# Flamingo block on one core: a table of its own for the last batch but one, a router without the softmax's sum, later weight splits and later reads of the counts

## The chip, the cores and the metric

The kernel is one program on one core of a Trainium2 chip. The metric is the device time of one execution in microseconds (us), as a median over several. Five engines work side by side: TensorE (PE, with its weight loads shown apart as PEld), VectorE (DVE), ScalarE (ACT), GpSimd (POOL) and SyncE (SP, which issues most DMAs). They wait for each other by semaphores alone.

## The reference, cut to what matters

Eight batches of 112 query rows (D = 256) go through four residual steps. `_L1_ffn_ref` is the part that the change touches most.

```python
x = x + tanh(g_xattn[0]) * _L0_xattn_ref(_layernorm(x), ctx, ...)   # 16 heads of 16
x = x + tanh(g_ffn[0]) * _L0_ffn_ref(_layernorm(x), ...)            # three matrices, tanh
x = x + tanh(g_xattn[1]) * _L1_xattn_ref(_layernorm(x), ctx, ...)   # 8 heads of 64, keys of x and ctx
x = x + tanh(g_ffn[1]) * _L1_ffn_ref(_layernorm(x), ...)            # 8 experts, 2 of them per row

def _L1_ffn_ref(hidden_states, gate_w, gate_up_proj, down_proj):
    probs = jax.nn.softmax(x @ gate_w.T, axis=-1)
    w, idx = jax.lax.top_k(probs, 2)
    w = w / jnp.sum(w, axis=-1, keepdims=True)
    ...   # for each expert: acc + ce * (silu(x @ g.T) * (x @ u.T)) @ dn.T
```

The two weights of a row are divided by their own sum, so the softmax's sum cancels in them.

## The kernel before, in words

`attention_order` writes out both attention layers as one list of stages. Each stage has a time in tables such as `PAIR`, `PREP1`, `TAIL1`, `TAIL_LAST` and `SPLIT`; the list is sorted by these times, and every engine walks the same list and does its share of each stage in that order. The times only set an order; nothing waits for a clock. A stage that comes early in the list and isn't ready holds up all that its engine has behind it.

In the second layer each batch has four pairs of heads. A pair is `S` (scores on PE, L667; maxima on DVE, L1034; exponentials on ACT, L1440), `sc` (POOL divides by the sums, all batches but the last), `T` (eight transposes on PE, L683; copies on ACT, L1140, and DVE, L1142) and `V` (values on PE, L701). The last batch is not divided before `V`: `rv` and `rb` (L712) bring the reciprocals of its sums, and `aT` (L1055) multiplies them in.

A tail follows each batch: `wo` (PE, L743), `res` (DVE, L1081 and L1087), `stats`, `norm` (DVE, L981, after POOL's rstd), `xt` (transposes, L482), `xtc` (ACT copy, L1318) and the router. The router is `rt0` (logits, L762), `rt1` (maximum and difference on DVE, exponential on ACT, L1476), `rt2` and `rt3` (one-hot rows `o1` and `o2` of the two best experts; each small DVE instruction waits for the one before through the semaphore `rchain`), `rt4` (weights on DVE; on PE the running places of the rows by a triangular and an all-ones matrix, L770 and L771) and `rt5` (row numbers `i1` and `i2` on DVE; two indirect DMAs on POOL, L1663, which scatter the 112 rows and their copy to the experts' places in DRAM). Every batch's tail but the last one's stands by `TAIL1` behind the last pair of its attention. So the tail of batch 6 (the last but one) lies among the four pairs of batch 7.

`keep_warm` puts spare transposes into PE's queue at fixed places (`WARM`): 18 ahead of the last `xt`, 26 ahead of the last `rt4`, 56 ahead of the first expert's `xin`.

The expert stage (`expert_order`) begins when all rows are scattered: SP waits for all the indirect DMAs, loads an expert's rows, PE transposes them (`xin`, L794), ACT and DVE make a high and a low half (L1493, L1227), and PE multiplies by weights that are split into high halves (ACT, L1566) and low halves (DVE, L1298, which reads the raw weights and the high half). Each expert has six such chunks. The six of expert 0 are split at the places of `SPLIT`; chunks 0 to 3 hold the first matrix, 4 and 5 the second. The weights of expert 0 are asked for by SP (L1780) behind the last `v1` of the attention. Each engine reads the number of rows of each expert from SBUF into registers (`count_of`, L863), for branches that handle more than 256 rows of an expert.

Of the kernel before, what the change touches and what calls it, by code (L numbers as in the profile page):

```python
# [10 lines left out]
ALU = mybir.AluOpType  # L11
ACT = mybir.ActivationFunctionType
AX = mybir.AxisListType
# [66 lines left out]
def emptied_by(stage, *i):  # L80
# [4 lines left out]
    if stage in ("kp", "v"):  # L85
# [45 lines left out]
         (33.31, "rt5"))  # L131
TAIL_LAST = ((1.58, "rv"), (4.84, "rb"), (6.92, "rbc"), (8.1, "aT"), (9.72, "wo"), (10.67, "res", 3),
# [3 lines left out]
SPLIT = ((4.0, 0), (4.72, 1), (6.9, 2), (15.65, 3), (15.74, 4), (22.13, 5))  # L136


WARM = {("kp", 0, 1, 0): 36, ("spk", 0, 0): 26, ("spk", 0, 2): 24, ("xt", NB - 1, 3): 18, ("rt4", NB - 1): 26, ("xin", 0): 56}


def attention_order():

    order, timed = Order(), []
    TQ, TP, TL = 5.5, 6.4, 4.4
    T1 = TQ * NQUAD + 4

# [36 lines left out]
    return order  # L186
# [53 lines left out]
def build(nc, A, out):  # L240
    ctx = ExitStack()
    with ctx:
# [102 lines left out]
        R = {n: sb("r_" + n, [NQ, NB, NE]) for n in ("p", "e1", "o1", "e2", "o2", "p2", "m", "t", "u")}  # L345
        r1 = {n: sb("q_" + n, [NQ, NB]) for n in ("mx", "z", "v1", "v2", "a", "b", "s1", "s2", "d")}
# [120 lines left out]
        def tensor_attention(e, w):  # L467
# [6 lines left out]
            for stage, *i in order.entries:  # L474
# [669 lines left out]
        def vector_route(e, w, stage, b):  # L1144
            r = {n: R[n][:, b, :] for n in R}
            q = {n: r1[n][:, b:b + 1] for n in r1}
            c = 24 * b
# [6 lines left out]
            elif stage == "rt2":  # L1154
                w.wait_ge(s("rexp"), b + 1)
                e.tensor_reduce(q["z"], r["u"], AX.X, ALU.add).then_inc(s("rchain"), 1)
                w.wait_ge(s("rchain"), c + 1)
                e.reciprocal(q["d"], q["z"]).then_inc(s("rchain"), 1)
                w.wait_ge(s("rchain"), c + 2)
                e.tensor_scalar(r["p"], r["u"], q["d"], None, ALU.mult).then_inc(s("rchain"), 1)  # L1160
                w.wait_ge(s("rconst"), 4)
                first_of(e, w, c + 3, r["p"], q["v1"], r["e1"], q["a"], r["o1"])
                w.wait_ge(s("rchain"), c + 7)
                e.scalar_tensor_tensor(r["p2"], r["o1"], -2.0, r["p"], ALU.mult, ALU.add).then_inc(s("rchain"), 1)
            elif stage == "rt3":
                first_of(e, w, c + 8, r["p2"], q["v2"], r["e2"], q["b"], r["o2"])
                w.wait_ge(s("rchain"), c + 12)
                e.tensor_tensor(r["m"], r["o1"], r["o2"], ALU.add).then_inc(s("rchain"), 1)
            elif stage == "rt4":
                e.tensor_tensor(q["s1"], q["v1"], q["v2"], ALU.add).then_inc(s("rchain"), 1)  # L1170
                w.wait_ge(s("rchain"), c + 14)
                e.reciprocal(q["s2"], q["s1"]).then_inc(s("rchain"), 1)
                w.wait_ge(s("rchain"), c + 15)
                for to, v in ((XN[:, b, :], "v1"), (XN2[b], "v2")):
                    e.scalar_tensor_tensor(to[:, D:D + 1], q[v], q["s2"], tg[0:NQ, 3:4], ALU.mult,
                                           ALU.mult).then_inc(s("rchain"), 1)
            else:
# [10 lines left out]
                at = c + 18  # L1188
# [9 lines left out]
        def first_of(e, w, at, src, v, eq, mx, oh):  # L1198

            w.wait_ge(s("rchain"), at)  # L1200
            e.tensor_reduce(v, src, AX.X, ALU.max).then_inc(s("rchain"), 1)
            w.wait_ge(s("rchain"), at + 1)
            e.scalar_tensor_tensor(eq, src, v, dec[:, :], ALU.is_equal, ALU.mult).then_inc(s("rchain"), 1)
            w.wait_ge(s("rchain"), at + 2)
            e.tensor_reduce(mx, eq, AX.X, ALU.max).then_inc(s("rchain"), 1)
            w.wait_ge(s("rchain"), at + 3)
            e.tensor_scalar(oh, eq, mx, None, ALU.is_equal).then_inc(s("rchain"), 1)

        def vector_experts(e, w):
# [9 lines left out]
            count = counts(e, w)  # L1219
            for stage, *i in moe.entries:  # L1220
# [8 lines left out]
                elif stage == "up":  # L1229
# [5 lines left out]
                                    ALU.mult).then_inc(s(f"pair{u % 3}"), 1)  # L1235
                elif stage == "hid":
# [23 lines left out]
                elif stage == "far":  # L1260
                    with e.If(count[NE] > 384):
# [216 lines left out]
        def scalar_experts(e, w):  # L1478
# [4 lines left out]
            count = counts(e, w)  # L1483
            for stage, *i in moe.entries:
# [10 lines left out]
                elif stage == "up":  # L1495
# [3 lines left out]
                    if n >= 2:  # L1499
                        w.wait_ge(s("hid"), n - 1)  # L1500
                    e.activation(SG[:, n % 2, :], ps[:, PAIRS[pair_use[(stage, x, dc)] % 3][0], :],  # L1501
                                 ACT.Silu).then_inc(s("silu"), 1)
                elif stage == "hid":
# [21 lines left out]
                elif stage == "far":  # L1525
                    with e.If(count[NE] > 384):
# [60 lines left out]
        def pool_attention(e, w):  # L1587
            for stage, *i in order.entries:
# [67 lines left out]
                elif stage == "rt5":  # L1656
# [4 lines left out]
                    for z, (i_, rows) in enumerate(((i1, XN[:, b, :]), (i2, XN2[b]))):  # L1661
                        w.wait_ge(s("rchain"), 24 * b + 21 + 3 * z)
                        e.indirect_dma_start(xs, bass.IndirectOffsetOnAxis(ap=i_[:, b:b + 1], axis=0), rows,  # L1663
                                             None).then_inc(s("scatter"), 16)
# [236 lines left out]
```

## Time and profile before

| | |
|---|---|
| runs | 632.99, 634.67, 635.07 us; median 634.67 |
| profiled execution | 632.88 us, its span 631.0 |
| busy share of the span | PE 92%, PEld 77%, DVE 63%, ACT 49%, POOL 45% |
| mean granted TensorE clock | 0.986 of full |
| order of time | first layer to about 212 us, second layer to about 437, last tails to about 459, experts to the end |

The span runs from the first to the last instruction that the profiler saw. A busy PE is not PE at its peak, since its matmuls overlap. The rows that the argument rests on stand in the section ahead of the prediction.

### The profile page before, as it was taken

To read this page: it belongs to the slowest core of one execution; us is meant where nothing else is said; L and a number is where in the kernel's file an instruction comes from. 1 tells how busy PE (TensorE), PEld (TensorE's weight loads), DVE (VectorE), ACT (ScalarE), POOL (GpSimd) and SP (SyncE) were. 2 spreads that over 40 slices of the span, in tenths; PEclk is the share of its full clock that TensorE was granted. 3 is DMA by queue.
4 is the path that set the end of the run, shared out by engine and by line. 5 is a ranking of instruction groups with operands and counts; after the bars stand their busy time and mean duration, and the time that the engine had idled before them with its cause. 6 is when DMAs were issued, how large, how long until landed. Compare 5 with 4: busy or idle time off the path is not lost.

```text
span 631.0 us, 13685 instructions
## 1 busy us (share of the span) xinstructions
PE 583.1 (92%) x5588; PEld 488.9 (77%) x5588; DVE 398.2 (63%) x809; ACT 309.1 (49%) x590; POOL 282.2 (45%) x240
## 2 busy tenths in 40 slices
PE   6779989999988999999999999987789999988994
PEld 5657666676756787878888787866679999987994
DVE  7564576677676465676756666577717777745761
ACT  2245545454544545554554546465125676635541
POOL 5967367558540045446546554630200443311224
PEclk9999999999989999999999999997989999999998
DMA  7900380000000000000000000045071776635111
GB/s 250 351 8 1 134 340 1 2 2 2 2 2 1 2 1 1 8 2 23 16 9 16 9 23 2 23 173 242 22 235 49 239 241 226 209 75 209 29 24 23
DMA packets 24170, 50.92 MB, mean 81 GB/s; under 512 B 7408, under 2 KB 16928, under 8 KB 20768
## 3 DMA queue, kind: packets, MB, share of 16 engines
q1 hardware_dynamic: 18784, 45.33, 20.0%
q0 software_dynamic: 4224, 3.70, 3.3%
q10 hardware_dynamic: 1088, 0.88, 0.5%
q8 instruction: 49, 0.80, 0.5%
q14 instruction: 25, 0.20, 0.1%
HBM read 37.89 MB, written 13.31 MB: 81 GB/s over the span
## 4 chain that ended last, share of the span: by engine, by line
PE 68%; POOL 14%; DVE 11%; ACT 3%; issue 2%; DMA 2%; SPq 0%; POOLq 0%; DVEq 0%; ACTq 0%
PE ps L58 13%; PE ps L60 12%; PE ps L59 12%; POOL sr L1612 11%; PE ps L701 4%; PE ps L667 4%; PE ps L683 4%; DVE KN L1009 4%; PE ps L633 2%; PE ps L647 2%; PE ps L623 2%; PE ps L542 2%; PE ps L561 2%; PE ps L743 2%; DMA WR<-in_gupT 1%
## 5 line engine op out<-in xcount | busy, mean ns | idle before, releaser
L1654 POOL TENSOR_SCALAR P<-P,rinv 112x487 f32<-112x487 f32 x56 | 85.6, 1539 | 63.2 <-DVE rinv L1042 63.0
L1612 POOL TENSOR_TENSOR sr<-sv,mhalf 125x32 f32<-125x32 f32 x16 | 87.0, 5437 | 1.3
L58 PE MATMUL ps<-XGf,WH 128*128 128x256 f32 x256 | 73.4, 287 | 2.8 <-ACT P L1559 1.4
L374 POOL DMA_INDIRECT out<-WS,rows_i x16 | 28.4, 1773 | 103.3 <-ACT WS L1514 99.3
L59 PE MATMUL ps<-XGf,WH 128*128 128x256 f32 x256 | 73.2, 286 | 0.0
L60 PE MATMUL ps<-XGf,WL 128*128 128x256 f32 x256 | 73.1, 286 | 0.0
L1009 DVE TENSOR_REDUCE KN<-ps 112x4 f32<-112x1500 f32 x32 | 55.0, 1719 | 26.3 <-PE ps L542 26.1
L1298 DVE TENSOR_TENSOR WL<-WR,WH 128x1024 fp32r<-128x1024 f32 x48 | 57.5, 1223 | 11.6 <-ACT WH L1566 11.5
L1440 ACT ACTIVATE P<-ps,nm 112x487 f32<-112x487 f32 x64 | 42.1, 663 | 45.3 <-DVE nm L1034 43.8
L1391 ACT ACTIVATE P<-ps 125x1344 f32<-125x1344 f32 x32 | 41.3, 1292 | 43.1 <-PE ps L561 43.1
L58 PEld LDWEIGHTS ps<-XGf,WH 128*128 128x128 f32 x256 | 49.8, 195 | 3.3 <-DVE XGf L1227 1.6
L1034 DVE TENSOR_REDUCE nm<-ps 112x1 f32<-112x487 f32 x64 | 39.3, 655 | 18.8 <-PE ps L667 18.8
L59 PEld LDWEIGHTS ps<-XGf,WH 128*128 128x128 f32 x256 | 49.9, 195 | 0.0
L60 PEld LDWEIGHTS ps<-XGf,WL 128*128 128x128 f32 x256 | 49.9, 195 | 0.0
L1566 ACT ACTIVATE WH<-WR 128x1024 fp32r<-128x1024 f32 x48 | 48.9, 1050 | 0.1
L1234 DVE TENSOR_TENSOR P<-P,ps 128x512 f32<-128x512 f32 x32 | 22.0, 687 | 38.1 <-PE ps L60 38.1
L58 PE MATMUL ps<-HTf,CS 128*125 128x256 f32 (+1 forms) x120 | 44.3, 369 | 0.0
L1018 DVE TENSOR_TENSOR KK<-ps,KK 128x487 fp32r<-128x487 f32 x32 | 21.2, 662 | 29.9 <-ACT KK L1408 29.9
L1501 ACT ACTIVATE P<-ps 128x512 f32<-128x512 f32 x32 | 19.1, 596 | 41.8 <-PE ps L60 41.8
L1599 POOL TENSOR_SCALAR ve<-mv 112x1 f32<-112x1 f32 x24 | 5.5, 231 | 75.7 <-DVE mv L974 75.7
L58 PE MATMUL ps<-WH,HTf 128*128 128x256 f32 x136 | 39.2, 289 | 0.0
L60 PE MATMUL ps<-HTf,CS 128*125 128x256 f32 (+1 forms) x120 | 39.2, 326 | 0.0
(233 smaller groups left out, 1530.1 us busy)
## 6 DMA issues: line engine op xcount, KB each, us to landing
WR<-in_gupT SPq DMA_DIRECT2D x16, 1024.0 KB, 7.2
WR<-in_dwnT SPq DMA_DIRECT2D x8, 1024.0 KB, 10.8
xs<-ZT SPq DMA_DIRECT2D x14, 516.0 KB, 5.8
P<-xs SPq DMA_DIRECT2D x24, 128.0 KB, 9.0
CT<-in_ctxT SPq DMA_DIRECT2D x1, 2250.0 KB, 10.1
Wk<-in_L_xattn_Wk SPq DMA_DIRECT2D x2, 512.0 KB, 10.5
Wv<-in_L_xattn_Wv SPq DMA_DIRECT2D x2, 512.0 KB, 11.0
out<-X SPq DMA_DIRECT2D x8, 112.0 KB, 1.9
```

The costliest lines, as they stand in the source:

```text
L58: e.matmul(out, ah, bh, start=start, stop=False)
L59: e.matmul(out, ah, bl, start=False, stop=False)
L60: return e.matmul(out, al, bh, start=False, stop=stop)
L374: return e.indirect_dma_start(result, rows, src, None, bounds_check=NT - 1, oob_is_err=False, compute_op=ALU.add)
L1009: e.tensor_reduce(heads(KN[b % 2][0:NQ, 3, :])[:, 4 * k:4 * k + 4, 16], ps[0:NQ, 0:4, 0:NC], AX.X, ALU.max, negate=True).then_inc(s("smax" ...
L1034: e.tensor_reduce(nm[:, k:k + 1], ps[0:NQ, z, 0:487], AX.X, ALU.max, negate=True).then_inc(s("nm"), 1)
L1298: e.tensor_tensor(WL[x % 3][:, cs], WR[x % 3][:, cs], f_(WH[x % 2][:, cs]), ALU.subtract).then_inc(s("wl"), 1)
L1391: e.activation(PQ[:, q % 3, :].rearrange("p (g n) -> p g n", g=4), ps[0:125, 0:4, 0:3 * NQ], ACT.Exp).then_inc(s("ex"), 1)
L1440: e.activation(P[:, k, 0:487], ps[0:NQ, z, 0:487], ACT.Exp, bias=nm[:, k:k + 1], accum_out=rsum[:, k:k + 1] if i[0] < LAST_A else rsum_las ...
L1566: e.activation(WH[x % 2][:, cs], WR[x % 3][:, cs], ACT.Copy).then_inc(s("wh"), 1)
L1612: e.tensor_tensor(sr[:, p, :], sv[:, p, :], mhalf[0:125, 0:32], ALU.pow).then_inc(s("sr"), 1)
L1654: e.tensor_scalar(P[:, k, 0:487], P[:, k, 0:487], rinv[:, k:k + 1], None, ALU.mult).then_inc(s("psc"), 1)
```

## The change

Four things change.

1. Batch 6 gets a table of its own, `TAIL_NEXT`: its `xt` and all of its router now stand behind the last `T` of batch 7, and `rt2`, `rt3` and DVE's part of `rt4` stand ahead of batch 7's `res`.
2. The router no longer sums the exponentials or divides by the sum. The best expert is where the difference to the maximum is 0, and its weight is 1, so `o1` needs only DVE. `m` = `o1` + `o2` is no longer made: PE adds the two in PSUM, by four matmuls where there were two. A batch has 19 steps in `rchain` where there were 24.
3. Chunks 3, 4 and 5 of expert 0 are split behind the last `rt5` on DVE, and behind the last exponential of the router on ACT.
4. DVE and ACT no longer read all nine counts ahead of the first expert. They read each one behind dc = 2 of its expert, as PE did already.

```diff
+TAIL_NEXT = ((12.96, "aT"), (14.41, "wo"), (16.12, "res", 3), (18.96, "stats", 3), (23.9, "norm", 3), (24.5, "xt", 3),
+             (25.0, "xtc", 3), (29.1, "rt0"), (29.15, "rt1"), (30.1, "rt2"), (30.2, "rt3"), (30.25, "rt4"),
+             (33.2, "rt5"))
-SPLIT = ((4.0, 0), (4.72, 1), (6.9, 2), (15.65, 3), (15.74, 4), (22.13, 5))
+SPLIT = ((4.0, 0), (4.72, 1), (6.9, 2), (38.0, 3), (38.1, 4), (38.2, 5))
...
-            for d, stage, *i in TAIL_LAST if last else TAIL1:
+            for d, stage, *i in TAIL_LAST if last else TAIL_NEXT if n == 2 * NB - 2 else TAIL1:
...
-                    w.wait_ge(s("rchain"), 24 * b + 13)
-                    e.matmul(ps[0:NQ, bk, 0:8], tri[:, :], R["m"][:, b, :], start=True, stop=True)
-                    t = e.matmul(ps[0:NQ, bk, 8:16], ones[:, :], R["m"][:, b, :], start=True, stop=True)
+                    w.wait_ge(s("rchain"), RC * b + 8)
+                    for cs, mat in ((slice(0, 8), tri), (slice(8, 16), ones)):
+                        for n in ("o1", "o2"):
+                            t = e.matmul(ps[0:NQ, bk, cs], mat[:, :], R[n][:, b, :], start=(n == "o1"), stop=(n == "o2"))
...
             elif stage == "rt2":
+                for sem_, v in emptied(("rt0", b)):
+                    w.wait_ge(sem_, v)
+                w.wait_ge(s("rconst"), 4)
+                e.scalar_tensor_tensor(r["e1"], r["t"], 0.0, dec[:, :], ALU.is_equal, ALU.mult).then_inc(s("rchain"), 1)
+                first_of(e, w, c + 1, r["e1"], q["a"], r["o1"])
+                w.wait_ge(s("rchain"), c + 3)
                 w.wait_ge(s("rexp"), b + 1)
-                e.tensor_reduce(q["z"], r["u"], AX.X, ALU.add).then_inc(s("rchain"), 1)
-                w.wait_ge(s("rchain"), c + 1)
-                e.reciprocal(q["d"], q["z"]).then_inc(s("rchain"), 1)
-                w.wait_ge(s("rchain"), c + 2)
-                e.tensor_scalar(r["p"], r["u"], q["d"], None, ALU.mult).then_inc(s("rchain"), 1)
...
-            count = counts(e, w)
+            count = []
...
+                    if dc == 2:
+                        count.append(count_of(e, w, x))
```

On DVE, behind the last batch's reciprocals, this stood before (S is the scratch that holds `rinv_last`, `rT` and `aT`; L1055 is `aT`, L1081 is batch 7's `res`, L1298 a split; the r_ and q_ names are batch 6's router):

```order
L1298 TENSOR_TENSOR WL<-WR,WH 128x1024 x2
L1151 TENSOR_REDUCE q_mx<-ps 112x1
L1153 TENSOR_SCALAR r_t<-ps,q_mx 112x8
L1142 COPY P<-ps 125x448
...
L1164 SCALAR_TENSOR_TENSOR r_p<-r_o,r_p 112x8
L1055 TENSOR_TENSOR S<-ps,S 128x448
...
L1168 TENSOR_TENSOR r_m<-r_o 112x8
L1298 TENSOR_TENSOR WL<-WR,WH 128x1024
L1081 TENSOR_TENSOR tt<-ps,bias 112x256
```

and this stands there in the changed kernel, whose lines are numbered a little higher (L1063 is `aT`, L1089 is `res`):

```order
L1150 COPY P<-ps 125x448
L1063 TENSOR_TENSOR S<-ps,S 128x448
L1162 TENSOR_REDUCE q_mx<-ps 112x1
L1164 TENSOR_SCALAR r_t<-ps,q_mx 112x8
L1170 SCALAR_TENSOR_TENSOR r_e<-r_t,dec 112x8
...
L1216 TENSOR_SCALAR r_o<-r_e,q_b 112x8
L1183 TENSOR_SCALAR q_s<-q_v 112x1
L1185 RECIPROCAL q_s<-q_s 112x1
L1187 TENSOR_SCALAR XN<-q_s,tg 112x1
L1188 SCALAR_TENSOR_TENSOR S<-q_v,q_s,tg 112x1
L1089 TENSOR_TENSOR tt<-ps,bias 112x256
```

The three splits are gone from here, the copy of the last transposes comes at once, and 14 small router instructions now stand between `aT` and `res`.

On PE, around batch 7's last transposes, before (L762 is batch 6's `rt0`; the lines L683 are the last pair's `T`, L712 is `rb`):

```order
L482 MATMUL ps<-ident,XN 128x112 x2
L762 MATMUL ps<-GW,XT 112x8 x2
L683 MATMUL ps<-ident,P 112x112
...
L712 MATMUL ps<-ident,S 128x112 x4
L701 MATMUL ps<-P,VV 64x112 x16
L743 MATMUL ps<-WO,S 112x256 x4
L770 MATMUL ps<-r_m,sq 112x8
```

and in the changed kernel (L488 is `xt`, L689 `T`, L707 `V`, L768 `rt0`, L749 `wo`, L779 `rt4`):

```order
L689 MATMUL ps<-ident,P 125x112 x3
L718 MATMUL ps<-ident,S 128x112 x4
L488 MATMUL ps<-ident,XN 128x112 x2
L707 MATMUL ps<-P,VV 64x112 x16
L768 MATMUL ps<-GW,XT 112x8 x2
L749 MATMUL ps<-WO,S 112x256 x4
L779 MATMUL ps<-r_o,sq 112x8 x4
```

Batch 6's `xt` and `rt0` moved from ahead of the last `T` to behind it, and `rt4` has four matmuls.

On DVE, behind the last `rt5` (L1208 is the cast to `i2`, L1222 the first of the counts, L1236 the first expert's low half), the changed kernel has:

```order
L1208 CAST i<-q_b 112x1
L1310 TENSOR_TENSOR WL<-WR,WH 128x1024 x3
L1222 TENSOR_TENSOR r_t<-base,ebase 112x8
L1224 CAST cnt<-r_t 112x8
L1225 TENSOR_REDUCE q_d<-r_t 112x1
L1227 CAST cnt<-q_d 112x1
L1236 TENSOR_TENSOR XGf<-ps,XGf 128x512
```

Before, the cast was followed at once by the counts. Now three splits stand between, with no wait in front of them.

## Rows read from the trace of the kernel before

**Rows 1.** The page: share of the span by engine in the chain.

```profile
PE 68%; POOL 14%; DVE 11%; ACT 3%; issue 2%; DMA 2%; SPq 0%; POOLq 0%; DVEq 0%; ACTq 0%
```

**Rows 2.** Windows: us, then busy of PE, PEld, DVE, ACT, POOL; clock; DMA.

```profile
300.00:350.00 50.00, 50.00 (x400) 41.21 (x397) 32.49 (x101) 25.66 (x60) 27.00 (x22) 1.00 0.05 15
```

**Rows 3.** Chain of waits, one inner batch's rt4: start us, us, what.

```profile
307.33 0.29 PE ps L770 x2
307.62 0.20 PE ps L771 x2
```

**Rows 4.** Chain of waits at the weights of expert 0: start us, us, what.

```profile
418.22 7.38 DMA WR<-in_gupT
...
427.85 0.67 DVE nm L1034
```

**Rows 5.** Timeline of PE in the last tails: start us, us, line, tile, shapes, records.

```profile
430.92 1.06 PE L683 MATMUL ps<-ident,P 112*112 112x112 f32 x8
431.91 0.99 PE L701 MATMUL ps<-P,VV 112*64 112x112 f32 x16
...
439.12 3.17 PE L701 MATMUL ps<-P,VV 112*64 112x112 f32 x32
443.02 1.98 PE L743 MATMUL ps<-WO,S 128*112 128x256 f32 x8 [0.73 <-DVE S L1055]
```

**Rows 6.** Timeline of ACT around the last exponentials.

```profile
433.08 0.54 ACT L1140 ACTIVATE P<-ps 125x448 f32<-125x448 f32 x1
...
435.40 0.36 ACT L1318 ACTIVATE XT<-ps 128x224 f32<-128x224 f32 x1
```

**Rows 7.** Timeline of DVE: aT and the first instruction of res.

```profile
442.34 0.62 DVE L1055 TENSOR_TENSOR S<-ps,S 128x448 f32<-128x448 f32 x1 [1.58 <-PE ps L701]
...
445.04 0.42 DVE L1081 TENSOR_TENSOR tt<-ps,bias 112x256 f32<-112x256 f32 x1
```

**Rows 8.** Windows of PE alone: busy, records, granted clock, DMA share, GB/s.

```profile
436.00:437.00 1.00, 1.00 (x6) 0.50 0.02 8
...
466.00:467.00 1.00, 1.00 (x7) 0.50 1.02 155
```

**Rows 9.** Timeline of DVE and PE: the router of batch 7.

```profile
449.91 0.23 DVE L1153 TENSOR_SCALAR r_t<-ps,q_mx 112x8 f32<-112x8 f32 x1
...
451.33 0.23 DVE L1203 SCALAR_TENSOR_TENSOR r_e<-r_p,q_v,dec 112x8 f32<-112x8 f32 x1
...
453.18 0.17 DVE L1168 TENSOR_TENSOR r_m<-r_o 112x8 f32<-112x8 f32 x1
...
449.53 3.04 PE L453 MATMUL ps<-ident 128*128 128x128 f32 x26
453.50 0.33 PE L770 MATMUL ps<-r_m,sq 112*112 112x8 f32 x2 [0.93 <-DVE q_s L1170]
```

**Rows 10.** Timeline of DVE, POOL and PE: from the row numbers to expert 0.

```profile
455.31 0.16 DVE L1213 TENSOR_TENSOR r_t<-base,ebase 112x8 f32<-112x8 f32 x1
...
455.62 0.94 POOL L1663 DMA_INDIRECT xs<-XN,i  x1 [3.76 <-DVE i L1195]
456.86 0.94 POOL L1663 DMA_INDIRECT xs<-S,i  x1 [0.30 <-issue]
...
462.29 0.44 PE L794 MATMUL ps<-ident,P 128*128 128x128 f32 x2 [1.53 <-DMA EX<-xs]
```

**Rows 11.** Timeline of POOL and DVE in the experts: scatters beside splits.

```profile
508.81 1.58 POOL L374 DMA_INDIRECT out<-WS,rows_i  x1 [10.46 <-ACT WS L1514]
510.69 2.24 POOL L374 DMA_INDIRECT out<-WS,rows_i  x1 [0.30 <-issue]
...
509.14 2.37 DVE L1298 TENSOR_TENSOR WL<-WR,WH 128x1024 fp32r<-128x1024 f32 x2 [1.21 <-ACT WH L1566]
```

**Rows 12.** One line's instructions (ns min/median/max), and a window of the experts.

```profile
L863 DVEq TENSOR_LOAD <-cnt x9: 298/309/559, 456.0 to 461.5; - x9
...
490.00:500.00 10.00, 10.00 (x86) 10.00 (x85) 7.91 (x11) 7.91 (x11) 6.57 (x4) 1.00 0.92 328
```

More of the change, by code:

```diff
@@ L343, in build @@
                ((XGf[:, 2560:3584], B["Wk2l"][:, :]), (HTf[:, 2048:3072], B["Wv2l"][:, :]))]
-        R = {n: sb("r_" + n, [NQ, NB, NE]) for n in ("p", "e1", "o1", "e2", "o2", "p2", "m", "t", "u")}
-        r1 = {n: sb("q_" + n, [NQ, NB]) for n in ("mx", "z", "v1", "v2", "a", "b", "s1", "s2", "d")}
+        R = {n: sb("r_" + n, [NQ, NB, NE]) for n in ("e1", "o1", "e2", "o2", "p2", "t", "u")}
+        r1 = {n: sb("q_" + n, [NQ, NB]) for n in ("mx", "v2", "a", "b", "s1", "s2", "d")}
         i1, i2 = sb("i1", [NQ, NB], U32), sb("i2", [NQ, NB], U32)
@@ L1146, in vector_route @@
             q = {n: r1[n][:, b:b + 1] for n in r1}
-            c = 24 * b
+            c = RC * b
             if stage == "rt1":
@@ new lines, in vector_route @@
+                w.wait_ge(s("rconst"), 4)
+                e.scalar_tensor_tensor(r["e1"], r["t"], 0.0, dec[:, :], ALU.is_equal, ALU.mult).then_inc(s("rchain"), 1)
+                first_of(e, w, c + 1, r["e1"], q["a"], r["o1"])
+                w.wait_ge(s("rchain"), c + 3)
+                w.wait_ge(s("rexp"), b + 1)
+                e.scalar_tensor_tensor(r["p2"], r["o1"], -2.0, r["u"], ALU.mult, ALU.add).then_inc(s("rchain"), 1)
+            elif stage == "rt3":
+                w.wait_ge(s("rchain"), c + 4)
+                e.tensor_reduce(q["v2"], r["p2"], AX.X, ALU.max).then_inc(s("rchain"), 1)
+                w.wait_ge(s("rchain"), c + 5)
+                e.scalar_tensor_tensor(r["e2"], r["p2"], q["v2"], dec[:, :], ALU.is_equal,
+                                       ALU.mult).then_inc(s("rchain"), 1)
+                first_of(e, w, c + 6, r["e2"], q["b"], r["o2"])
@@ L1169, in vector_route @@
             elif stage == "rt4":
-                e.tensor_tensor(q["s1"], q["v1"], q["v2"], ALU.add).then_inc(s("rchain"), 1)
-                w.wait_ge(s("rchain"), c + 14)
+                e.tensor_scalar(q["s1"], q["v2"], 1.0, None, ALU.add).then_inc(s("rchain"), 1)
+                w.wait_ge(s("rchain"), c + 9)
                 e.reciprocal(q["s2"], q["s1"]).then_inc(s("rchain"), 1)
[L1173 to L1176, printed above, removed]
+                w.wait_ge(s("rchain"), c + 10)
@@ L1177, in vector_route @@
+                e.tensor_scalar(XN[:, b, D:D + 1], q["s2"], tg[0:NQ, 3:4], None, ALU.mult).then_inc(s("rchain"), 1)
+                e.scalar_tensor_tensor(XN2[b][:, D:D + 1], q["v2"], q["s2"], tg[0:NQ, 3:4], ALU.mult,
+                                       ALU.mult).then_inc(s("rchain"), 1)
             else:
@@ L1187, in vector_route @@
                                 ALU.add).then_inc(bank_sem("rt4", b), 1)
-                at = c + 18
+                at = c + 13
                 for oh, s_, i_ in ((r["o1"], q["a"], i1), (r["o2"], q["b"], i2)):
@@ L1196, in vector_route, with first_of @@
                     at += 3
-        def first_of(e, w, at, src, v, eq, mx, oh):
+        def first_of(e, w, at, eq, mx, oh):
             w.wait_ge(s("rchain"), at)
-            e.tensor_reduce(v, src, AX.X, ALU.max).then_inc(s("rchain"), 1)
+            e.tensor_reduce(mx, eq, AX.X, ALU.max).then_inc(s("rchain"), 1)
             w.wait_ge(s("rchain"), at + 1)
[L1203 to L1206, printed above, removed]
             e.tensor_scalar(oh, eq, mx, None, ALU.is_equal).then_inc(s("rchain"), 1)
@@ L1260, in vector_experts @@
                 elif stage == "far":
+                    count.append(count_of(e, w, NE))
                     with e.If(count[NE] > 384):
@@ L1482, in scalar_experts @@
             w.wait_ge(s("rt4"), NB)
-            count = counts(e, w)
+            count = []
             for stage, *i in moe.entries:
@@ L1502, in scalar_experts @@
                                  ACT.Silu).then_inc(s("silu"), 1)
+                    if dc == 2:
+                        count.append(count_of(e, w, x))
                 elif stage == "hid":
@@ L1525, in scalar_experts @@
                 elif stage == "far":
+                    count.append(count_of(e, w, NE))
                     with e.If(count[NE] > 384):
@@ L1661, in pool_attention @@
                     for z, (i_, rows) in enumerate(((i1, XN[:, b, :]), (i2, XN2[b]))):
-                        w.wait_ge(s("rchain"), 24 * b + 21 + 3 * z)
+                        w.wait_ge(s("rchain"), RC * b + 16 + 3 * z)
                         e.indirect_dma_start(xs, bass.IndirectOffsetOnAxis(ap=i_[:, b:b + 1], axis=0), rows,
```

8 lines of the change are left out of this document (1 added, 7 removed).

## The prediction

> **What bounds the kernel now.** I read the page first. Its chain of the work that ended last is two thirds PE [rows 1], but such a share is a mean over stages, so I asked for windows. Across the second layer PE is busy for the whole of each window and the others are not [rows 2]; the reader sees 50.00 of 50.00 for PE, 32.49 for DVE and 27.00 for POOL. What PE gets more to do there is paid in full. Then I followed the chain of waits piece by piece from 404 us on. At 418.22 PE drops out of it: the load of expert 0's weights takes 7.38 us, ACT and DVE split a chunk of it, and only then come the maxima of a pair, at 427.85 [rows 4]. That load is asked for behind PE's last `v1`, so it moves with PE. From there to the experts the chain alternates between engines, a string of latencies in which a removed wait is a gain. In the experts PE is full again [rows 12].
>
> **The tail of batch 6 (a gain of 4.3 us).** Last exponentials done, ACT copies the previous pair from 433.08 to 433.62, and that copy is the last thing the final `T` needs. But ahead of it in PE's queue stand batch 6's `xt` and `rt0`, and on ACT two splits stand ahead of the copy that `rt0` needs, so that copy begins only at 435.40 [rows 6]. All of this is the wait that the new order removes. PE also runs at half its clock here: 0.50, the level of 1.2 GHz, in the window at 436 [rows 8], behind these waits. `V` shows it: two pairs take 3.17 us for 32 records, where one pair took 0.99 for 16 at full clock, so 1.98 for two [rows 5].
>
> In the new order `T` starts at 433.7. At full clock its eight transposes take 1.0 us and the six behind it (`rb` four, `xt` two) 0.75 at the same rate [rows 5]; with `V` at 1.95 this ends at about 437.3. I assume full clock, since PE then idles only 0.8 us, from the end of `V` at 432.9 [rows 5] to 433.7. The copies and reciprocals that it needs from DVE and ACT have no split in front of them any more. `aT` starts at 437.3 and not at 442.34 [rows 7]: 5.0 us earlier.
>
> Not all of it is kept. Before, `res` started 2.70 us behind the start of `aT` [rows 7], about when `wo` was done, 0.68 + 1.98 behind it [rows 5]; the router steps and a split filled that time on DVE. Now 14 router instructions stand there. Those of batch 7 give their pace: from `r_e` at 451.33 to `r_m` at 453.18 are 8 steps, 0.23 each [rows 9]. Ten such are 2.3 us; the last four wait less for each other, and I take 0.6 for them. With 0.55 for `aT` that is 3.45 in all instead of 2.70. So `res` starts at 440.75 and not at 445.04 [rows 7]: 4.3 us earlier. From `res` to the last `rt0` nothing changes. Bounds: if the clock falls all the same, 1.2 us more for `V`, so 3.1; if the small steps were no longer than `wo`, 5.0.
>
> **The router of batch 7 (a gain of 0.55 us).** `e1` can now follow `r_t` at 450.17 instead of 451.33, which is 1.16 us, and PE waits for `o2` and no longer for `m`, a step of 0.19 behind it: 1.35 us in all [rows 9]. PE can't use all of it. Its 26 spare transposes run from 449.53 to 452.57, while `rt4` began at 453.50 [rows 9]. So 0.95 us is gained there at most, and two matmuls more at 0.20 each give 0.4 back.
>
> **Four matmuls for two (a loss of 2.0 us).** In an inner batch `rt4` takes 0.29 + 0.20 us in the chain [rows 3]: the second matmul, 112 rows by 8 columns, costs 0.20 though it computes almost nothing. Two more per batch are 0.4 us. Batches 0 to 4 pay it while PE is the bound [rows 2]: 5 x 0.4 = 2.0. Batch 5's lies behind the last `v1` and beside the 7.38 us load [rows 4], batch 6's ahead of 18 spare transposes; both are hidden. DVE's five steps fewer per batch gain nothing, since DVE isn't the bound here. Bounds: 1.0 if the repeated matrix costs half, 2.5 if each costs what a half of the 0.49 is.
>
> **Splits in the gap before the experts (a loss of 1.9 us).** DVE has nothing to do from the counts until the first expert's rows are there, so three splits seem free: 3.5 us by their row of two in 2.37 [rows 11], in the 7 us from 455.31 to 462.29 [rows 10]. But POOL issues the last two scatters in the same gap, at 455.62 and 456.86 [rows 10], and every row of expert 0 waits for them. Scatters beside splits have rows in the experts. The one at 508.81, before a split began, took 1.58. The one at 510.69, begun while the second of two splits ran (509.14 to 511.51), took 2.24 [rows 11]: 0.66 more, most of what was left of that split. So a split in progress holds a scatter back until it ends. Laid onto the new order, in the old times: the splits start at 455.31, where the first step of the counts stood [rows 10], and again at 456.45 and 457.6. The first scatter comes at 455.62, is held to 456.4 and ends at 457.35; the second comes 0.30 later at 457.65, just behind the start of the third split, and is held to 458.75. Before it ran at 456.86: 1.9 us later.
>
> The Trainium skill (page "SBUF — State Buffer", section "Who interferes with whom") speaks against this place: a VectorE instruction with two inputs in SBUF contends with a GpSimd instruction that reads SBUF, and the loser blocks for the whole instruction. By that rule, the trace agrees: the lengthened scatters are those that meet a split. The same section also says that its own probe saw `tensor_tensor` not stall a DMA; by this the term would be 0 and the sum 1.9 lower, and the row of 2.24 speaks against it.
>
> **The clock at the experts' start (a loss of 0.5 us).** PE's spare transposes end 1.53 us before the first rows come [rows 10], and a little later the clock is at 0.50 for a few us of dense matmuls [rows 8]. With 1.9 us more of idle time PE starts the experts slow rather than falls slow on the way. I take 0.5 from between 0 (the slow stretch only moves) and 1.5 (it lasts twice as long).
>
> **The counts (0).** Nine reads stood in the same gap, 0.3 us each and 5.5 us from the first to the last [rows 12]; with the splits there they would end after the first rows' arrival, so their move is what pays for the splits' move. In the experts one read costs DVE 0.7 us (5.5 / 8) per expert, and DVE is idle for a fifth of a window there [rows 12]. It reads behind the product of dc = 2, and the next half that PE needs is due one `up` later.
>
> **The sum** is made against the profiled execution (632.88 us): -4.3 - 0.55 + 2.0 + 1.9 + 0.5 = -0.45. That execution lies 1.8 us below the median of the runs, 634.67, so I put the difference on the median: **634.2 us**.
>
> **Rivals.**
> - *Only the first scatter is held.* The second would come 0.02 to 0.12 us behind the start of the third split, which is close; if it gets in first, the loss is 0.8 and the clock's 0.3: -1.75, 632.9 us. For it: the margin. Against: the times as laid out above put it behind.
> - *No scatter is held.* Then -2.85, 631.8. Only the row of 2.24 speaks against it, and that row's scatter adds into the output, another form.
> - *The extra matmuls are free*, since two of the four use a matrix just loaded: -2.45, 632.2. Against: the 0.20 of the second matmul.
> - *POOL does not get in between the splits* (the other side). They follow each other without a wait. No row shows a scatter that arrives in the first of several. If it is held until all three are over, at 458.75, the second scatter starts at 460.0, 3.1 us late, and the clock costs the full 1.5: +1.75, 636.4. It decides from the point where the first scatter has not begun before 456.45. The Trainium skill (same page, section "SBUF: two separate sides") says there are deep queues that would have to be drained to share; by that this rival would be the outcome, and I give it a seventh.
> - *The clock falls in the last attention too*: +1.2, so +0.75, 635.4.
>
> **How the numbers follow.** Forecast 35 in 100, first scatter only 25, starved POOL 15, none held 10, free matmuls 8, clock in the tail 7. What a measurement can tell from no change is about 0.3%, 1.9 us. The forecast and the tail clock lie within it; the first-only case lies at its edge and gives half of its chance to faster; none held and free matmuls are faster; the starved case is half slower. With some spread on each: faster 0.34, same 0.50, slower 0.16. The range runs from none held, with the gain a little above, to the starved case: 631.4 to 636.6.
>
> **What would show it.** In the changed kernel's profile: the last `T` within 1 us of the last exponentials and a granted clock of 1.00 at the two `V`s; `res` 4 to 5 us earlier against the last maxima; the four matmuls of the last `rt4` in 0.9 us and a distance from the first to the sixth `rt4` that is 2.0 us longer; PE's `rt4` of batch 7 straight behind the spare transposes; the first scatter of batch 7 longer than 1.5 us and the second longer than 1.9. If the scatters take 0.94 the term of 1.9 is wrong; if the last `v1` comes no later than before, the 2.0 is wrong; if DVE's counts make PE wait in an expert, the 0 is.

## The result, and the profile after

The changed kernel takes 637.07 us (median of 12 runs, 635.36 to 638.67), the kernel before 634.57 us beside it (12 runs, 632.43 to 637.53). The ratio is 1.0040, with a 95% interval of 1.0024 to 1.0056: 2.5 us slower, where 0.5 us faster was forecast and the range ended at 636.6. The top of its page, whose rows answer to [rows 1]:

```profile
span 635.1 us, 13717 instructions
PE 588.7 (93%) x5620; PEld 492.9 (78%) x5620; DVE 391.0 (62%) x769; ACT 308.6 (49%) x590; POOL 287.8 (45%) x240
PEclk9979999999999999999999999999979999989998
PE 70%; POOL 13%; DVE 10%; ACT 3%; issue 2%; DMA 1%; SPq 0%; POOLq 0%; DVEq 0%; ACTq 0%
```

The shares tell little: PE is busy for 93% as before. The clock line has a 7 in the third of its 40 slices (from 32 us on), a 7 in the 30th, where the experts start, and an 8 in the 36th, in the overflow of expert 4. All three come up again below.

**The last attention** (PE's timeline; V is L707, T is L689, `wo` is L749) answers to [rows 5 to 7]:

```profile
436.32 0.99 PE L707 MATMUL ps<-P,VV 112*64 112x112 f32 x16
438.14 1.03 PE L689 MATMUL ps<-ident,P 112*112 112x112 f32 x8 [0.83 <-ACT P L1148]
439.67 1.76 PE L707 MATMUL ps<-P,VV 112*64 112x112 f32 x32
442.16 1.98 PE L749 MATMUL ps<-WO,S 128*112 128x256 f32 x8 [0.24 <-DVE S L1063]
```

The last T follows 0.5 us behind the last exponentials, which end at 437.6, and the two V take 1.76 us for 32 records instead of 3.17. The granted clock is 1.00 there, that is 2.4 GHz, where it was 0.50. This part came as forecast. A window while V runs:

```profile
440.00:441.00 1.00, 1.00 (x26) 1.00 (x24) 0.00 (x0) 0.87 (x3) 0.00 (x0) 1.00 0.06 25
```

**From the last rt4 to the experts** (the chain of waits: start, us, what) answers to [rows 9, 10]:

```profile
452.29 0.71 PE ps L779 x8
453.02 0.17 DVE r_u L1198
...
454.58 4.00 POOL xs L1678
458.58 0.30 issue
458.88 2.58 DMA xs<-S,i
...
462.79 1.76 DMA EX<-xs
464.60 0.70 PE ps L802 x2
```

One line stands out. The scatter on POOL took 4.00 us where the same instruction took 0.94. DVE's timeline beside it:

```profile
454.28 3.49 DVE L1310 TENSOR_TENSOR WL<-WR,WH 128x1024 fp32r<-128x1024 f32 x3
```

The scatter starts 0.30 us behind the first of three splits, which begin 1.13 us apart, and ends 0.81 us behind the last. The second scatter follows at 458.88 and not, as laid out, while a split ran.

**The overflow of expert 4** wasn't in the argument at all. Windows of the changed kernel (PE, PEld, DVE, ACT, POOL busy, then the granted clock):

```profile
467.00:468.00 1.00, 1.00 (x6) 1.00 (x7) 0.00 (x0) 0.00 (x0) 0.00 (x0) 0.50 0.71 209
566.00:567.00 1.00, 1.00 (x4) 0.77 (x3) 0.00 (x0) 0.00 (x0) 1.00 (x1) 0.55 0.86 88
567.00:568.00 1.00, 1.00 (x4) 0.79 (x3) 0.00 (x0) 0.00 (x0) 0.51 (x1) 0.50 0.29 43
```

The first of these is the slow stretch at the experts' start, which the kernel before has too [rows 8]. The other two are new: PE falls to half clock in the overflow, the branch for the rows of expert 4 beyond 256, behind two idle stretches (0.76 us ahead of its first transposes L898, 1.01 behind them) that have the same lengths before. (In the changed kernel's repeats, e11 and e12, the first is 0.85.) A window of the kernel before at the same place:

```profile
564.00:565.00 1.00, 1.00 (x6) 0.83 (x5) 0.00 (x0) 0.00 (x0) 1.00 (x1) 1.00 1.09 123
```

The slow stretch at the experts' start isn't the same in both either. Windows of the changed kernel, then of the kernel before:

```profile
464.00:465.00 1.00, 0.83 (x4) 0.32 (x3) 0.00 (x0) 0.00 (x0) 0.00 (x0) 0.50 0.54 118
```

```profile
464.00:465.00 1.00, 0.28 (x2) 0.28 (x3) 0.67 (x1) 0.00 (x0) 0.01 (x1) 1.00 0.72 110
```

One less the granted clock, added up over the windows of 1 us there, gives 1.7 us in each execution of the kernel before and 3.4 in each of the changed one: 3.4 and 6.8 us at 0.50.

**Where the time went.** Each kernel was profiled three times in all (e6, e7, e11 and e12 below are the repeats), so a stage's length can be told from its scatter. Means of three, in us ("overflow" below is the last row but one, from the first transposes of that branch to its next ones):

| from ... to | before | after | difference | predicted |
|---|---|---|---|---|
| start, first `rt4` | 280.00 | 281.70 | +1.70 | 0 |
| first load of expert 0's weights | 138.29 | 140.25 | +1.96 | +2.0 |
| `X` of batch 7's `res` | 27.24 | 23.20 | -4.04 | -4.3 |
| `r_u` of batch 7 | 8.56 | 7.80 | -0.76 | -0.55 |
| last scatter | 2.80 | 5.86 | +3.06 | +1.9 |
| first expert matmul | 7.72 | 7.96 | +0.24 | +0.5 |
| first transposes of the overflow (L898) | 96.81 | 96.92 | +0.11 | 0 |
| next transposes in it (L911) | 7.00 | 8.62 | +1.62 | 0 |
| end | 62.60 | 62.81 | +0.21 | 0 |

The lengths agree within 0.1 us among a kernel's three executions in the rows for the load, `r_u`, the scatter and the overflow. The first row is PE's clock, ahead of anything that the change alters on PE. Over all sixteen profiled executions of this study the first `rt4` starts between 279.5 and 283.5. I added up one less the granted clock over the 28 windows of 10 us ahead of it: with 1.7 us lost it starts at 279.5 (two executions), with 3.4 at 280.2 or 280.3 (four), with 5.1 or 5.2 at 281.3 to 282.1 (seven), with 6.8 at 282.0 and 282.4, with 8.6 at 283.5. Without it the profiles differ by 2.4 us, and the medians by 2.5. The kernel before has a median 1.7 us above its three profiled executions (632.82 to 632.92), the changed one 0.1. A median execution of the kernel before thus has a lower clock than its profiled ones: 0.980 of full over the 33 executions beside e1 to e4, where the three profiled ones have 0.983 to 0.986; the changed kernel has 0.981 over its 12 and 0.980 to 0.981 in its three.

### The profile page after: what moved, and what is told of

Read it like the earlier page. It is cut to its first block, busy times and chain, and to the rows that moved or that the text cites. A ratio compares the mean times of both kernels' runs of the same rounds, so it can differ in the third digit from the quotient of the medians.

```text
span 635.1 us, 13717 instructions
## 1 busy us (share of the span) xinstructions
PE 588.7 (93%) x5620; PEld 492.9 (78%) x5620; DVE 391.0 (62%) x769; ACT 308.6 (49%) x590; POOL 287.8 (45%) x240
## 4 chain that ended last, share of the span: by engine, by line
PE 70%; POOL 13%; DVE 10%; ACT 3%; issue 2%; DMA 1%; SPq 0%; POOLq 0%; DVEq 0%; ACTq 0%
PE ps L58 13%; PE ps L59 12%; PE ps L60 12%; POOL sr L1627 10%; PE ps L707 4%; PE ps L673 4%; PE ps L689 4%; DVE KN L1017 4%; PE ps L639 2%; PE ps L548 2%; PE ps L653 2%; PE ps L629 2%; PE ps L567 2%; PE ps L749 2%; PE ps L583 1%
## 5 line engine op out<-in xcount | busy, mean ns | idle before, releaser
L1669 POOL TENSOR_SCALAR P<-P,rinv 112x487 f32<-112x487 f32 x56 | 87.7, 1579 | 58.0 <-DVE rinv L1050 57.8
L59 PE MATMUL ps<-WL,HTf 128*128 128x256 f32 x136 | 38.4, 283 | 0.0
```

What stands on the lines that cost most here:

```text
L59: e.matmul(out, ah, bl, start=False, stop=False)
L1669: e.tensor_scalar(P[:, k, 0:487], P[:, k, 0:487], rinv[:, k:k + 1], None, ALU.mult).then_inc(s("psc"), 1)
```

## The experiments

Fourteen runs. A median is beside the kernel before on the same chip, with the ratio's 95% interval.

### e1: the splits wait for the scatters

```diff
         w.wait_ge(s("wh"), 6 * x + c + 1)
+        if x == 0 and c >= 3:
+            w.wait_ge(s("scatter"), 32 * NB)
         e.tensor_tensor(WL[x % 3][:, cs], WR[x % 3][:, cs], f_(WH[x % 2][:, cs]),
```

> The changed kernel, but DVE's last three splits of expert 0 wait until all scatters of the router have landed. Theory A (the three splits hold the first scatter of batch 7 back until the last of them is over; it took 4.00 us where 0.94 was enough): both scatters take 0.94 again, r_u to the second scatter shrinks from 5.86 to 2.8 us, the experts start 3.0 us earlier, 634.0 us. Theory B (the 4.00 us are not the splits' doing, but for instance the scatter's own wait for its row data or for code): the scatter stays long and the time stays at 637.1. Theory C (the scatters come early, but the splits, now 3.5 us long behind the landing, end after expert 0's rows have come and DVE is late for the rest of the rows): 634.5 to 636.

634.12 us, 0.9983 (0.9965 to 1.0001) of before: 3.0 us less than the changed kernel. POOL and DVE in its timeline:

```profile
454.13 0.94 POOL L1680 DMA_INDIRECT xs<-XN,i  x1 [3.00 <-DVE i L1208]
455.37 0.94 POOL L1680 DMA_INDIRECT xs<-S,i  x1 [0.30 <-issue]
458.07 3.50 DVE L1312 TENSOR_TENSOR WL<-WR,WH 128x1024 fp32r<-128x1024 f32 x3 [4.16 <-DMA xs<-S,i]
```

Both scatters take 0.94, and the distance from `r_u` to the second is 2.79. Theory A. The starvation is the splits' doing, and it costs 3.0 us of 637. No other stage of this trace differs from the changed kernel's by more than 0.4.

### e2: two matmuls in rt4 again

```diff
-                    for cs, mat in ((slice(0, 8), tri), (slice(8, 16), ones)):
-                        for n in ("o1", "o2"):
-                            t = e.matmul(ps[0:NQ, bk, cs], mat[:, :], R[n][:, b, :], start=(n == "o1"), stop=(n == "o2"))
+                    for cs, mat in ((slice(0, 8), tri), (slice(8, 16), ones)):
+                        t = e.matmul(ps[0:NQ, bk, cs], mat[:, :], R["m"][:, b, :], start=True, stop=True)
...
+                e.tensor_tensor(r["m"], r["o1"], r["o2"], ALU.add).then_inc(s("rchain"), 1)
```

> The changed kernel, but with the sum of the two choices formed on DVE as before and two matmuls in rt4 instead of four, in all batches. Theory A (each of the two extra matmuls costs PE 0.2 us and batches 0 to 4 pay for it): the load of expert 0's weights is issued 1.9 us earlier relative to the first rt4, 635.2 us. Theory B (the two extra are nearly free, and the later load in the profile has another cause): 637 us.

635.09 us, 1.0000 (0.9978 to 1.0023): 2.0 less. From the first `rt4` to the load it takes 138.29 us, the value of before, and 1.96 less than in the changed kernel. That shows the price; that the medians give the same is partly luck. This trace also gains 0.4 at `r_u` and 1.6 in the overflow (7.01 us), and loses 0.7 in the last attention and 1.1 between the last scatter and the overflow, with more time at half clock in both. The sixth `rt4` in its chain of waits, then in the changed kernel's:

```profile
420.38 0.31 PE ps L778 x4
```

```profile
422.01 0.70 PE ps L779 x8
```

Each matmul has two records here, so x4 are two matmuls. Two more cost 0.39 us, and five batches pay. That two of the four use a matrix just loaded saves nothing.

### e3: the tail's new table alone

The kernel before with `TAIL_NEXT` and nothing else.

> The kernel before, with the new times for the tail of the last batch but one and nothing else. Theory A (the tail's gain is 4.7 us, as read in the profile, and nothing takes it back): PE at full clock in the last attention, 630.0 us. Theory B (the three splits that keep their old times stand in front of the copies in this tail too, so that only part is gained): 631 to 633. Theory C (each gain of idle time is paid back by a lower clock afterwards): 634.

638.41 us, 1.0065 (1.0038 to 1.0091): none of the three theories. It is 3.7 us slower than before. DVE, then PE, in its timeline:

```profile
437.17 2.36 DVE L1301 TENSOR_TENSOR WL<-WR,WH 128x1024 fp32r<-128x1024 f32 x2 [0.70 <-ACT WH L1569]
439.45 0.41 DVE L984 TENSOR_SCALAR XN<-X,mv,rstd 112x256 f32<-112x256 f32 x1
```

```profile
437.16 0.55 PE L715 MATMUL ps<-ident,S 112*128 112x112 f32 x4
439.91 0.64 PE L485 MATMUL ps<-ident,XN 112*128 112x112 f32 x2 [2.21 <-DVE XN L984]
440.48 3.26 PE L704 MATMUL ps<-P,VV 112*64 112x112 f32 x32
```

The splits that kept their old places now stand on DVE between the reciprocals and batch 6's `norm`. PE waits 2.21 us for `XN` in front of the last V, and V then runs at half clock. From the load to batch 7's `X` it takes 30.36 us, 3.1 more than before. The slow overflow (8.61 us) is in this trace too.

### e4: the splits and the counts alone

The kernel before with the new `SPLIT` and the counts read in the experts.

> The kernel before, with the three splits moved behind the attention and the counts read in the experts, and nothing else. Theory A: the scatters of batch 7 are held through the three splits, +3.1 us; ACT and DVE lose two splits each in front of the copies of the last attention's tail, which gives 0 to 2.3 us back, 1.8 taken: 635.9 us (bounds 635.4 to 637.7). Theory B (the splits don't hold the scatters when the router is the old one): 632.8. Theory C (the counts read in the experts make PE wait there): a gap of PE in an expert, and over 638.

637.22 us, 1.0049 (1.0027 to 1.0071). From `r_u` to the last scatter 5.86, as in the changed kernel. And from the load to `X` 24.42 us: moving the splits alone, under the old table, gives 2.8 of the 4.0 us of the tail. Theory A holds at the scatters; its 635.9 lacks 1.3, and this trace has the slow overflow too (8.59), which no theory had. PE in its timeline:

```profile
437.07 0.38 PE L482 MATMUL ps<-ident,XN 112*128 112x112 f32 x2 [1.50 <-DVE XN L981]
437.90 0.56 PE L762 MATMUL ps<-GW,XT 128*112 128x8 f32 x4 [0.45 <-ACT XT L1321]
438.31 1.04 PE L683 MATMUL ps<-ident,P 112*112 112x112 f32 x8
439.19 0.55 PE L712 MATMUL ps<-ident,S 112*128 112x112 f32 x4
439.67 1.76 PE L701 MATMUL ps<-P,VV 112*64 112x112 f32 x32
```

Batch 6's `xt` and `rt0` still stand ahead of T. Without a split in front of their copies they cost little, and the clock stays up for V. So the two edits aren't separate terms. The new table gives 1.2 us on top of moved splits and takes 3.1 without them. The counts cost nothing that shows: the five experts up to the overflow take 96.81 us in the kernel before and 96.92 in the changed one. No run moves the counts alone.

### e5: both costs taken out

The edits of e1 and e2 together.

> The changed kernel with both costs taken out: DVE's last three splits wait for the router's scatters, and the sum of the choices is formed on DVE with two matmuls in rt4. If the two act apart from each other, as e1 (3.0 us off) and e2 (2.0 us off) suggest: 637.1 - 3.0 - 2.0 = 632.1 us. Rival: PE's clock takes part of it back, since the first matmuls of the experts then meet another moment of its fall and rise: 633 to 634.

630.27 us, 0.9931 (0.9906 to 0.9955), from 7 runs: 4.4 us faster than before by the ratio. That is 1.8 better than the sum of the two medians, but only 0.8 better by the ratios (0.9983 + 1.0000 - 1.0040 = 0.9943), which lies inside the interval, so the two costs add up as far as this can tell. The fast overflow (7.02 us in its trace, 7.01 in e2's, 8.59 in e1's) is no gain on top of the sum: e2 has it already.

### e8: spare transposes in front of the first matmul

```diff
-WARM = {..., ("rt4", NB - 1): 26, ("xin", 0): 56}
+WARM = {..., ("rt4", NB - 1): 26, ("xin", 0): 56, ("up", 0, 0): 12}
```

This is on top of e5; the twelve write to a free bank.

> As e5, with 12 spare transposes more on PE between the transposes of expert 0's first rows and its first matmul, where PE idles 1.5 us while ACT and DVE split the rows. Theory A (the idle time there lets the clock fall, 12 matmuls at half clock cost 1.1 us in e1): full clock for the experts' first matmuls, 1.1 us less than e5. Theory B (the fall is decided by the idle time that lies ahead of the rows, and 12 transposes at half clock take 2.6 us and hold the first matmul up): 1.2 us more than e5.

630.05 us, 0.9914 (0.9889 to 0.9939), from 6 runs; its median is that of e5. Windows of e8, then of e5:

```profile
447.00:448.00 1.00, 1.00 (x6) 1.00 (x5) 0.86 (x6) 1.00 (x2) 0.47 (x1) 0.50 0.17 52
461.00:462.00 1.00, 1.00 (x10) 1.00 (x10) 0.00 (x0) 0.00 (x0) 0.00 (x0) 1.00 0.79 217
```

```profile
461.00:462.00 1.00, 1.00 (x6) 1.00 (x6) 0.00 (x0) 0.00 (x0) 0.00 (x0) 0.50 0.95 248
```

At the experts' start theory A holds in this trace: full clock, and from the first matmul to the next expert's rows 8.74 us instead of 11.10. But the same execution has a stretch at half clock among the spare transposes ahead of the last `rt4`, where e5 has none (`X` to `r_u` 9.08 us against 7.42), and one in the overflow (8.59 against 7.02). Whether the one fall causes the others is not shown; the median didn't move.

### e6 and e7: the kernel before, twice more

> The kernel before once more, unchanged, for another profiled execution of it. Theory A (its profiled execution of 632.88 us met fewer falls of PE's clock than most, at the start and in the tile of the overflow): the first rt4 starts at about 281.5 and not 279.5, and the overflow takes 8.6 us from the end of expert 4 to the next expert's rows as in most traces of the changed kernels; time 634 to 635. Theory B (the changed order itself makes the clock fall there): 279.5 and 7.0 again.

> The kernel before a third time, unchanged, with the same two theories as for its second profiled execution: start and overflow vary from execution to execution (A), or belong to the order of the work (B).

632.82 and 632.92 us. First `rt4` at 280.28 and 280.20, overflow 7.01 and 7.00. For the overflow that is theory B; the start lies between the two theories.

### e9: two splits in the gap

```diff
+        if x == 0 and c == 5:
+            w.wait_ge(s("scatter"), 32 * NB)
```

> The changed kernel, but of DVE's last three splits of expert 0 two run in the gap and the third waits until the scatters have landed. Theory A (a scatter that meets a row of splits waits until the whole row is over, and then takes 0.8 us more): in the changed kernel the three splits took 3.49 us and the scatter ended 0.81 behind them; with two, 2.35 us long, it takes 2.9 us instead of 4.0, and the second follows 1.1 us earlier: 636.0 us. Theory B (it waits for a fixed time, or for one split only): 4.0 us as with three, or 1.8.

636.08 us, 1.0042 (1.0017 to 1.0068), 1.0 less than the changed kernel. POOL and DVE:

```profile
454.81 2.86 POOL L1680 DMA_INDIRECT xs<-XN,i  x1 [3.00 <-DVE i L1208]
457.98 0.94 POOL L1680 DMA_INDIRECT xs<-S,i  x1 [0.30 <-issue]
```

```profile
454.51 2.35 DVE L1312 TENSOR_TENSOR WL<-WR,WH 128x1024 fp32r<-128x1024 f32 x2
```

The scatter ends at 457.67, 0.81 us behind the two splits, as it ended 0.81 behind three. Theory A, to the hundredth, at the scatters: from `r_u` to the last one 4.73 us, 1.13 less. That the median fits too is partly luck, since this trace also has the fast overflow (7.01) and loses 0.8 between the last scatter and the overflow.

### e10: the splits apart

```diff
+        if x == 0 and c >= 4:
+            w.wait_ge(s("wl"), 6 * x + c)
```

Each of the last two splits waits until the one before has been written.

> The changed kernel, with each of the last two splits of expert 0 on DVE waiting until the split before it has been written, so that DVE's three splits don't overlap at their ends. Theory A (POOL can't get in because the next split is already under way when one ends; a pause of about 0.1 us lets it in): the first scatter takes 1.8 to 2.1 us, the second is held by a later split, together 1 to 2 us earlier: 635 to 636. Theory B (so short a pause doesn't matter, the later split still comes first): 4.1 to 4.2 us for the first scatter, 637.2 us.

634.57 us, 1.0011 (0.9984 to 1.0039): 2.5 us less than the changed kernel by the medians, 1.8 by the ratios. Theory A had 1 to 2 us, and the first scatter's 1.73 lies just below its 1.8 to 2.1. From `r_u` to the last scatter it takes 3.59 us: 2.27 of the 3.06 are back, without taking a split out of the gap. POOL and DVE:

```profile
453.01 1.73 POOL L1680 DMA_INDIRECT xs<-XN,i  x1 [3.00 <-DVE i L1208]
455.04 1.02 POOL L1680 DMA_INDIRECT xs<-S,i  x1 [0.30 <-issue]
```

```profile
452.71 3.87 DVE L1312 TENSOR_TENSOR WL<-WR,WH 128x1024 fp32r<-128x1024 f32 x3
```

The splits now start 1.32 us apart and last 1.22, so there is 0.1 us between them. The first scatter ends 0.81 us behind the end of the first split (453.93), with the second split already running from 454.03. The second starts at 455.04 in the second split, which ends at 455.26, and ends 0.80 behind it, while the third split runs from 455.36. So the pause is enough: a scatter held by a split goes through at the first moment when DVE has no split under way. Not all of the gain reaches the experts in this execution: the second scatter lands 3.76 us behind its start and not 2.58. In e14, with the same pause, it is 2.67.

### e11 and e12: the changed kernel, twice more

> The changed kernel once more, unchanged, for another profiled execution. Theory A (its later start, first rt4 at 281.8 against 279.5, 280.3 and 280.2 in three of the kernel before, is chance): about 280.2 this time, and a time near 635.5. Theory B (it belongs to the order): 281.8 again. For the overflow: 8.6 us if it belongs to the order, 7.0 if it is chance.

> The changed kernel a third time, unchanged, with the same theories as for its second profiled execution.

636.96 and 636.98 us. First `rt4` at 281.40 and 281.92, first scatter 4.00 us in both, overflow 8.60 and 8.64. The scatter and the overflow repeat to some hundredths. The starts speak for theory B as far as three can: all late, though not in the same way (two lose the clock between 30 and 50 us, e11 between 180 and 200). But e10, with the changed kernel's stages up to there, starts at 280.21, and e3 and e4, with the old ones, at 281.40 and 282.02, so the stages ahead don't fix it. Whether the changed kernel starts late more often than the one before, or three executions fell so, is open.

### e13: the overflow's idle stretches filled

```diff
                         pairs_out(w, x)
+                        for _ in range(6):
+                            e.transpose(ps[:, 0, 0:128], ident[:, :], ident[:, :])
...
             t.then_inc(pe, 1)
+            for _ in range(8):
+                e.transpose(ps[:, 0, 0:128], ident[:, :], ident[:, :])
             w.wait_ge(dve, 5 * k + 1)
```

> The changed kernel with 6 and 8 spare transposes on PE in the two places of the overflow tile where PE idles 0.76 and 1.01 us. Theory A (these two stretches let the clock fall there): PE stays at full clock, the overflow takes 7.0 us again and not 8.6, and the time is 635.5. Theory B (the fall is owed to something else, for instance to what came before): still 8.6 us at half clock, 637.1, or more, since the transposes then take twice as long.

636.01 us, 1.0026 (1.0008 to 1.0044), 1.1 less than the changed kernel where 1.6 was expected. Its overflow takes 7.01 us, and its windows there are at full clock:

```profile
566.00:567.00 1.00, 0.86 (x7) 0.62 (x5) 0.42 (x1) 0.19 (x1) 1.00 (x1) 1.00 0.23 45
567.00:568.00 1.00, 1.00 (x6) 0.79 (x5) 0.00 (x0) 0.00 (x0) 0.69 (x2) 1.00 0.47 94
```

This fits theory A. It isn't proof, since e2, e5, e9 and e10 go through the unfilled overflow in 7.0 us too, while e1, e3, e4 and e8 take 8.6. The idle stretches don't decide the fall alone; whether it needs them isn't shown by the two filled kernels (e13 and e14) that go without it.

### e14: all in one kernel

The edits of e2, e10 and e13.

> The changed kernel with the sum of the choices formed on DVE and two matmuls in rt4, with each of DVE's last two splits of expert 0 waiting for the one before it, and with the spare transposes in the overflow. If the three gains add up: 637.1 - 2.0 - 2.5 - 1.6 = 631.0 us. Rivals: the spare transposes give nothing, 632.6; as good as or better than e5 (630.3), since DVE's splits are over before the rows come: 630.

631.79 us, 0.9949 (0.9931 to 0.9968): 3.2 us faster than before by the ratio; the sum promised 631.0. The overflow takes 7.02 us, the scatters 1.73 and 1.02. e5 needs no spare transposes and is as good, within the intervals.

## Why the prediction was wrong

- **What failed: "a split in progress holds a scatter back until it ends".** As put, the scatter would get in at the end of the split that it met, 456.4 in the old times. It got in at the end of the row of three. The row of before that I used [rows 11] couldn't tell the two apart: its scatter met the last split of a row, and so did the four others of that trace that started beside two splits. The term was +1.9 and measured +3.06. The rival that I gave a seventh, POOL starved through all three splits, happened, at its own price of 3.1; its 636.4 in all still lies below the measured 637.07. e1 takes it away, e9 shortens it by one split, and e10 shows the reason: splits that follow each other without a pause overlap by 0.09 us and leave no moment between them. The sentence of the Trainium skill cited there (page "SBUF — State Buffer", section "SBUF: two separate sides") says that whichever of the two engines starts first has the shared ports for the whole instruction, and that deep queues would have to be drained to share them. That the hold goes on across a row of instructions it doesn't state; the trace shows it with 4.00, 2.86 and 1.73 us for three, two and one split to wait for. The other sentence that the prediction cites (same page, section "Who interferes with whom"), that a probe saw `tensor_tensor` not stall a DMA, doesn't hold for this pair: the same three figures speak against it.
- **What was missing: a term for the overflow, +1.6.** I looked for the clock where the change put idle time, at the experts' start, and took the dense stretches behind as fixed. The overflow of expert 4 has idle stretches of 0.76 and 1.01 us in both kernels, and whether the clock falls there differs between kernels and, in the three executions of each that were profiled, not between executions of one (7.00 to 7.01 before, 8.60 to 8.64 after). With this term and the starved one the forecast of -0.45 becomes +2.3. What sets the clock's fall there stays open.
- **The tail (-4.3, measured -4.04):** right in size, wrong in cause. "All of this is the wait that the new order removes" holds only together with the moved splits: the splits' move alone gives 2.8 (e4), the new table alone costs 3.1 (e3). The sum held since both edits were in.
- **The router (-0.55, measured -0.76)** and **four matmuls for two (+2.0, measured +1.96, taken out again by e2):** right, by their own steps. The rival of free matmuls is out.
- **The clock at the experts' start (+0.5):** +0.24 up to the first matmul, +0.06 behind. PE does start the experts slow. The slow stretch lasts twice as long, 6.8 us for 3.4, which was the prediction's case of 1.5. It costs little, since its first half lies over PE's idle time and over the transposes of the first rows (0.69 us instead of 0.44); of the dense matmuls it covers 3.2 to 3.9 us where it covered 3.4. The 0.5 came close by a choice between two cases, and neither of them describes this.
- **The counts (0):** nothing shows, +0.11 up to the overflow.
- **The median.** I put the difference on a median 1.8 us above the profiled execution. The changed kernel's median lies 0.1 above its three, so part of that distance belonged to the kernel before alone. It goes with the mean clock: of the kernel before beside e5, executions with 0.988 took 632.03 and 632.42 us, one with 0.973 took 637.40. Where an execution that wasn't profiled lost its clock isn't on record.

## What to carry to other kernels

A gap of VectorE isn't free if GpSimd issues indirect DMAs in it: ask whose instructions fall into the gap. If long two-input instructions of VectorE must go there, let each wait for the one before, which cost 0.1 us a piece here and gave back 2.3 us at the scatters. A median that moves by the forecast amount doesn't confirm the step by itself: the traces of e2 and e9 show gains and losses elsewhere of 0.8 to 2 us, and only the stage's own length showed the step. A row of the trace in which a wait ends with an instruction doesn't tell whether it would have ended with the next one too; look for one that met the first of a row, or bound the cost by the whole row. And edits to an order should be tried apart before each gets a term of its own, since one may be a loss without the other.

## What the runs showed of the hardware

A scatter of 112 rows issued by POOL (0.94 us alone) beside DVE's 128 x 1024 subtractions with both inputs in SBUF ends 0.81 us behind the end of the unbroken row of them: 4.00 us with three, 2.86 with two, 1.73 with one. A pause of 0.1 us on DVE lets it in. The scatters that add into the output, in the experts of the kernel before, take 1.55 us alone; the five that start in the second of two splits take 2.12 to 2.26 and end 1.41 to 1.44 behind that split, while those that start 0.20 to 0.34 us ahead of a row of two take 1.55 to 1.64. So it counts which of the two starts first. In both forms the time from the end of the splits to the end of the scatter is about 0.13 us less than the scatter takes alone.

PE's granted clock falls to 0.50, the level of 1.2 GHz, in places that differ between kernels with the same idle stretches, and repeats within a kernel at one such place (overflow 7.0 or 8.6 us) but not at another (the kernel before loses 1.7 or 3.4 us of clock ahead of its first `rt4`). Over the sixteen profiled executions the loss there goes from 1.7 to 8.6 us and the first `rt4` from 279.5 to 283.5, so 1.7 us lost moves the rest by about 1.0. Keeping it up in one place (e8, 2.36 us gained at the experts' start) came with falls in two others in that execution, and the median stayed at e5's.
